# Wavelet attention: split lanes in both partition halves, and the row maxima as products of their own

## The reference, cut to what matters

```python
xe, xo = x[:, 0::2], x[:, 1::2]
a   = (xe + xo) * inv                      # (B, 1024, 128)
q   = (a @ wq).reshape(B, L, nh, hd)       # nh = 16 heads, hd = 8
k   = (a @ wk).reshape(B, L, nh, hd)
v   = (a @ wv).reshape(B, L, nh, hd)
att = einsum('bqhd,bkhd->bhqk', q, k) * (1 / sqrt(hd))
att = softmax(att, axis=-1)
o   = einsum('bhqk,bkhd->bqhd', att, v)
```

## Time and profile before

| | us |
|---|---|
| median of 3 runs | 4333.51 (4330.52 to 4335.92) |
| the profiled execution | 4323.26 |
| its span, first to last instruction | 4321.9 |
| TensorE busy, products | 3622.4 (84% of the span) |
| VectorE busy | 3291.8 (76%) |
| ScalarE busy | 2847.1 (66%) |
| GpSimd busy | 1003.8 (23%) |

### The profile page before, as it was taken

One profiled execution on the slowest core, in us unless ns is written; L12 is line 12 of the kernel. 1 busy time (PEld: TensorE's weight loads), 2 busy tenths in 40 slices (PEclk: granted clock), 3 DMA queues, 4 the chain that ended last, 5 costly groups with the idle time before them and its releaser, 6 DMA issues.

```text
span 4321.9 us, 74465 instructions
## 1 busy us (share of the span) xinstructions
PE 3622.4 (84%) x28950; PEld 1915.9 (44%) x28950; DVE 3291.8 (76%) x5099; ACT 2847.1 (66%) x4856; POOL 1003.8 (23%) x1479
## 2 busy tenths in 40 slices
PE   6999869998899998999996666666666659899999
PEld 4666522222444445676674122221122215566666
DVE  6787768886301137788886999999999996778887
ACT  3655416656334444666665999999999995566665
POOL 2444432100576630000002232322322220000000
PEclk8999959999999998999997555555555559899999
DMA  1000033330521000000001011111110110000000
GB/s 49 1 1 1 1 56 58 64 54 11 117 41 39 20 20 6 14 4 12 2 2 23 16 22 23 22 23 22 22 22 15 22 20 21 7 12 7 17 2 12
DMA packets 256877, 97.51 MB, mean 23 GB/s; under 512 B 223859, under 2 KB 241918, under 8 KB 256510
## 3 DMA queue, kind: packets, MB, share of 16 engines
q1 hardware_dynamic: 256526, 92.74, 10.8%
HBM read 31.75 MB, written 2.23 MB: 8 GB/s over the span
## 4 chain that ended last, share of the span: by engine, by line
PE 41%; DVE 29%; issue 12%; ACT 6%; DMA 1%; POOL 0%; SPq 0%; DVEq 0%; ACTq 0%; POOLq 0%
DVE d_negmax L2838 14%; PE psum L2364 7%; PE psum L2393 6%; DVE f_m_E L2463 6%; PE psum L2379 6%; PE psum L2063 5%; PE psum L2085 5%; ACT d_junk L2896 3%; PE psum L1447 2%; PE psum L1435 2%; DVE wl_negmax L1571 2%; DVE f_pT_E L2482 2%; PE psum L1424 2%; ACT wl_p L1712 1%; DVE residual L2493 1%
## 5 line engine op out<-in xcount | busy, mean ns | idle before, releaser
L2838 DVE TENSOR_REDUCE d_negmax<-psum 128x1 f32<-128x1024 f32 x1024 | 1171.5, 1214 | 25.5 <-PE psum L2774 23.4
L2896 ACT ACTIVATE d_junk<-psum,d_negmax 128x1024 bf16<-128x1024 f32 x1024 | 1136.8, 1126 | 37.0 <-DVE d_negmax L2838 32.6
L2774 PE MATMUL psum<-d_qT,d_kT 64*128 64x512 bf16 x2048 | 622.9, 604 | 432.7 <-ACT d_junk L2896 415.5
L2557 ACT ACTIVATE hidden<-psum,f_nm_E 128x1024 f32<-128x1024 f32 x512 | 566.5, 1113 | 143.5 <-DVE f_nm_E L2466 143.4
L2463 DVE TENSOR_REDUCE f_m_E<-psum 128x1 f32<-128x1024 f32 x512 | 602.1, 1218 | 46.8 <-PE psum L2364 45.5
L2364 PE MATMUL psum<-f_k_E,f_q_swapped_E 64*128 64x512 f32 x1024 | 527.2, 625 | 6.6 <-ACT hidden L2557 6.6
L2364 PE MATMUL psum<-f_k_E,f_q_E 64*128 64x512 f32 x1024 | 527.0, 624 | 2.9 <-DVE f_v_E L2454 2.0
L2564 ACT COPY f_pT_E<-psum 128x512 f32<-128x512 f32 x512 | 299.9, 586 | 323.8 <-PE psum L2379 323.8
L2393 PE MATMUL psum<-f_pT_E,f_v_E 128*64 128x128 f32 x8192 | 506.5, 277 | 2.5 <-DVE residual L2493 2.5
L2774 PEld LDWEIGHTS psum<-d_qT,d_kT 64*128 64x128 bf16 x2048 | 108.3, 101 | 843.1 <-ACT d_junk L2896 761.4
L2482 DVE COPY f_pT_E<-psum 128x512 f32<-128x512 f32 x512 | 351.6, 687 | 159.4 <-PE psum L2379 149.8
(11 more groups left out here) (331 smaller groups left out, 4720.9 us busy)
## 6 DMA issues: line engine op xcount, KB each, us to landing
moe_gates_on_all<-moe_gate_spill SPq DMA_DIRECT2D x16, 1024.0 KB, 11.8
f_q_swapped_E<-f_q_E SPq DMA_DIRECT2D x64, 128.0 KB, 2.3
moe_w<-in_moe_w SPq DMA_DIRECT2D x15, 256.0 KB, 6.5
residual<-in_hidden_states SPq DMA_DIRECT2D x2, 768.0 KB, 8.1
out<-residual SPq DMA_DIRECT2D x1, 1024.0 KB, 5.4
wl_qT<-wl_q_rows SPq DMA_TRANSPOSE x48, 3.3
residual<-in_hidden_states SPq DMA_DIRECT2D x2, 256.0 KB, 3.2
m_taps<-in_m_conv SPq DMA_DIRECT2D x4, 128.0 KB
```

What stands on the lines that cost most here:

```text
L2557: A.activation(pb[:, u % 2, f * 2 * BANK:(f + 1) * 2 * BANK], two(2 * f), ACT.Exp, bias=nm[:, u % 4:u % 4 + 1], scale=SC, accum_out=rs[:, ...
L2774: last = T.matmul(bank(2 + 2 * (at % 3) + jj), kT[half, s, jb * P:(jb + 1) * P], qT[half, s, hf * BANK:(hf + 1) * BANK], start=True, stop= ...
L2838: V.tensor_reduce(mh[:, t % 2, n // 2, n % 2:n % 2 + 1], two(2 + 2 * (at % 3)), X, ALU.max, negate=True).then_inc(*maxed.up(at))
L2896: A.activation(junk[:, at % 3, :], two(2 + 2 * (at % 3)), ACT.Exp, bias=mh[:, t % 2, n // 2, n % 2:n % 2 + 1], accum_out=sh[:, t % 2, n // ...
```

## The change

The ninth pair of parts (the two lowest, 2 and 2) is left out: `TERMS` has the eight pairs with i + j < 4, and `ROWS` is 64. The rows of q and k are laid out twice, in partitions 0 to 63 and 64 to 127 (index `r`), so `spread` makes 16 copies for q and 16 for k. The q rows have one buffer instead of two. In `pe_max` the first product of 512 columns takes the lower half, the second the upper half. In `pe_exp` the two products do the same and are left open, and two more products add the maxima: bf16 ones on three lanes against three lanes of `mT`, in the 32-partition group `(hh + 2 * j) % 4`, the two products of a unit in groups of opposite halves. The maxima's parts have their own tile `um`, which `dve_shift` fills (three small copies in place of one, to give the later half of the tokens a rotated order of heads) and `sp_shifted` transposes with one transposition into `mT`, two buffers. `dve_shift` no longer waits for the round's row transpositions but for the transposition of the maxima of the round before. GpSimd's memsets at the start fill other tiles. The waits follow: `pe_exp` waits once in a round for the maxima's lanes, `spread` for the row transpositions of the round before for q and k alike.

```diff
-        NG, HD, NH, ROWS = 9, 8, 16, 75
+        HD, NH, ROWS = 8, 16, 64
+        TERMS = [(i, j) for i in range(3) for j in range(3) if i + j < 4]
...
-                uq = sb(st, "wl_q_rows", [P, 2, 4, CT, P], BF16)
-                uk = sb(st, "wl_k_rows", [P, 4, CT, P], BF16)
+                uq = sb(st, "wl_q_rows", [P, 4, CT, 2, len(TERMS), HD], BF16)
+                uk = sb(st, "wl_k_rows", [P, 4, CT, 2, len(TERMS), HD], BF16)
+                um = sb(st, "wl_max_rows", [P, CT, 4, 32], BF16)
+                mT = sb(st, "wl_mT", [P, 2, B2], BF16)
+                onesb = sb(st, "ones_bf16", [P, P], BF16)
...
                     SP.wait_ge(*max_rows(b, g))
-                    if n:
-                        SP.wait_ge(*second_pass(*rounds_c[n - 1], 0, 3))
-                    for hh in range(4):
-                        SP.dma_start_transpose(in_lanes(qT[n % 3][:, hh]), in_blocks(uq[:, n % 2, hh])).then_inc(*shifted[hh].one())
+                    if n >= 2:
+                        SP.wait_ge(*second_pass(*rounds_c[n - 2], CT - 1, 3))
+                    SP.dma_start_transpose(in_lanes(mT[:, n % 2]), um[:, :, :, :].rearrange("p t g c -> p (t g c)")).then_inc(*shifted.one())
...
                     for j in range(2):
-                        last = T.matmul(bank(bk + j), qT[n % 3][0:ROWS, h % 4, i * P:(i + 1) * P], kT[n % 3][0:ROWS, h % 4, j * BANK:(j + 1) * BANK],
+                        half = slice(ROWS * j, ROWS * j + ROWS)
+                        last = T.matmul(bank(bk + j), qT[n % 3][half, h % 4, i * P:(i + 1) * P], kT[n % 3][half, h % 4, j * BANK:(j + 1) * BANK],
                                         start=True, stop=True)
...
                     for j in range(2):
-                        last = T.matmul(bank(bk + j), kT[n % 3][0:ROWS, hh, kt * P:(kt + 1) * P], qT[n % 3][0:ROWS, hh, j * BANK:(j + 1) * BANK], start=True, stop=True)
+                        half = slice(ROWS * j, ROWS * j + ROWS)
+                        T.matmul(bank(bk + j), kT[n % 3][half, hh, kt * P:(kt + 1) * P], qT[n % 3][half, hh, j * BANK:(j + 1) * BANK],
+                                 start=True, stop=False)
+                    for j in range(2):
+                        lanes = slice(32 * ((hh + 2 * j) % 4), 32 * ((hh + 2 * j) % 4) + 3)
+                        last = T.matmul(bank(bk + j), onesb[lanes, :], mT[lanes, n % 2, j * BANK:(j + 1) * BANK], start=False, stop=True)
...
-                    for i in range(3):
+                    for i, j in TERMS:
...
-                        for j in range(3):
-                            last = e.tensor_copy(u[:, :, :, i, j, :] if w == "q" else u[:, :, :, j, i, :], src)
+                        for r in range(2):
+                            last = e.tensor_copy(u[:, :, :, r, 3 * i + j, :], src)
...
-                    vstep(V.tensor_copy(mrest[:, :, :], negm[:, :, hs]))
-                    group_rows(V, round_at[b, g])
-                    places = uq[:, round_at[b, g] % 2].rearrange("p h t c -> p t h c")
+                    near, far = slice(0, CT // 2), slice(CT // 2, CT)
+                    V.tensor_copy(mrest[:, near, :], negm[:, near, hs])
+                    V.tensor_copy(mrest[:, far, 0:2], negm[:, far, 4 * g + 2:4 * g + 4])
+                    vstep(V.tensor_copy(mrest[:, far, 2:4], negm[:, far, 4 * g:4 * g + 2]))
+                    if round_at[b, g]:
+                        V.wait_ge(*max_turned(round_at[b, g] - 1))
```

More of the change, by code:

```diff
@@ L1292, in phase_C @@
                 turned = [loads(f"wl_turned_{n}") for n in range(2)]
-                shifted = [loads(f"wl_shifted_rows_{n}") for n in range(4)]
+                shifted = loads("wl_shifted_rows")
                 round_at = {r: n for n, r in enumerate(rounds_c)}
@@ L1302, in group_rows, with max_turned @@
                         e.wait_ge(*rows(n, hh))
-                def q_again(n, hh):
-                    return shifted[hh].sem, 16 * (n + 1)
+                def max_turned(n):
+                    return shifted.sem, 16 * (n + 1)
                 first_pass = signal("scored", at("max"))
@@ L1310, in phase_C @@
                 max_rows = signal("wl_max_rows", rounds_c)
+                lanes_set = signal("wl_lanes_set", range(1))
                 second_pass = signal("wl_shifted", at("exp"))
@@ L1326, in phase_C @@
                 in_lanes = lambda t: t.rearrange("p (t n) -> p t n", n=P)
-                in_blocks = lambda u: u.rearrange("p t c -> p (t c)")
+                in_blocks = lambda u: u.rearrange("p t r e x -> p (t r e x)")
                 def sp_rows(b, g):
@@ L1336, in sp_rows @@
                         arrived = turned[n % 2] if n else first_turned[hh]
-                        SP.dma_start_transpose(in_lanes(qT[n % 3][:, hh]), in_blocks(uq[:, n % 2, hh])).then_inc(*arrived.one())
+                        SP.dma_start_transpose(in_lanes(qT[n % 3][:, hh]), in_blocks(uq[:, hh])).then_inc(*arrived.one())
                         SP.dma_start_transpose(in_lanes(kT[n % 3][:, hh]), in_blocks(uk[:, hh])).then_inc(*arrived.one())
@@ L1429, in pe_exp @@
                     n = round_at[b, g]
-                    if kt == 0:
-                        T.wait_ge(*q_again(n, hh))
+                    if kt == 0 and hh == 0:
+                        T.wait_ge(*max_turned(n))
                     pe_av_behind(quad_at[b, g, kt], hh)
@@ L1523, in spread @@
                         e.wait_ge(*parted(b, 1, 2))
[L1524 to L1528, removed]
+                    if n:
                         group_rows(e, n - 1)
-                    u = (uq[:, n % 2] if w == "q" else uk[:, :, :, :])[:, :, :, 0:MR].rearrange("p h t (i j x) -> p h t i j x", i=3, j=3)
-                    for i in range(3):
+                    u = (uq if w == "q" else uk)[:, :, :, :, :, :]
+                    for i, j in TERMS:
                         cs = slice(D * (w == "k") + 4 * HD * g, D * (w == "k") + 4 * HD * (g + 1))
-                        src = part[:, i, :, cs].rearrange("p t (h x) -> p h t x", x=HD)
-                        for j in range(3):
-                            last = e.tensor_copy(u[:, :, :, i, j, :] if w == "q" else u[:, :, :, j, i, :], src)
+                        src = part[:, i if w == "q" else j, :, cs].rearrange("p t (h x) -> p h t x", x=HD)
+                        for r in range(2):
+                            last = e.tensor_copy(u[:, :, :, r, 3 * i + j, :], src)
                     return last
@@ L1575, in dve_shift @@
                     V.wait_ge(*maxed(b, 4 * g + 3, CT - 1))
-                    vstep(V.tensor_copy(mrest[:, :, :], negm[:, :, hs]))
-                    group_rows(V, round_at[b, g])
-                    places = uq[:, round_at[b, g] % 2].rearrange("p h t c -> p t h c")
+                    near, far = slice(0, CT // 2), slice(CT // 2, CT)
[4 more added lines that the diff above has]
+                        V.wait_ge(*max_turned(round_at[b, g] - 1))
+                    else:
+                        V.wait_ge(*lanes_set(0))
                     for n in range(3):
-                        last = V.tensor_copy(places[:, :, :, MR + n], mrest[:, :, :])
+                        last = V.tensor_copy(um[:, :, :, n], mrest[:, :, :])
                         if n < 2:
                             vstep(last)
-                            vstep(V.tensor_tensor(mrest[:, :, :], mrest[:, :, :], places[:, :, :, MR + n], ALU.subtract))
+                            vstep(V.tensor_tensor(mrest[:, :, :], mrest[:, :, :], um[:, :, :, n], ALU.subtract))
                     last.then_inc(*max_rows.up(b, g))
@@ L1736, in pool @@
                     enter(G)
-                    G.memset(uq[:, :, :, :, MR:P], 0.0)
-                    gstep(G.memset(uk[:, :, :, MR:P], 0.0))
+                    G.memset(onesb[:, :], 1.0)
                     for v in vp:
                         G.memset(v[:, :, :, HD:HD + 1], 1.0)
-                    gstep(G.memset(uk[:, :, :, MR:MR + 3], 1.0))
+                    G.memset(um[:, :, :, :], 0.0).then_inc(*lanes_set.up(0))
+                    G.wait_ge(*lanes_set(0))
                     for kind, *u in seq:
```

1 line of the change is left out of this document (removed).

## The result

| | before | after |
|---|---|---|
| median, 20 executions each on one chip | 4332.67 us | 4340.45 us |
| ratio, 95% interval | | 1.0017 (1.0011 to 1.0024) |
| span of the profiled execution | 4321.9 | 4339.9 |
| TensorE busy, products | 3622.4 | 3611.6 (83%) |
| GpSimd busy | 1003.8 | 1032.3 (24%) |

The change costs 7.8 us of the median, 0.17%, just inside what I called the same; the forecast was 10 us. The profiled pair differs by 18 us. Of these, 3.4 were there when the phase began (VectorE's first memset at 563.27 us instead of 559.88), which the change doesn't touch, and 4 came after its last copy of wl_oT; 10.4 us lie between these two marks.

What follows compares the result with a forecast made beforehand. The prediction took a quad's cycle of three E, three M, two AV and one maximum as the bound. It summed 1.2 + 4.2 + 2.4 + 2.4 = +10.2 us to 4344 us, range 4313 to 4385.

Steps and rivals of the forecast that it cites:

- what I called the same: Whole kernel: a measurement can tell about 0.2% from no change, 8.7 us; chance of landing within it 0.26.
- 40 quads: Five of eight wavelet attention rounds, four heads of one key tile each: 6.28 us against 6.25, together +1.2 us.
- last round, 8 quads: Last round, no M beside E: layout changes raise TensorE to 4.74 us against ScalarE's 4.21, together +4.2 us.
- copies at the start: Start of the phase: q and k layout copies grow from 9 to 16 each, seven more at 0.35 us, +2.4 us.
- maxima's lanes, 8 rounds: VectorE's step for each round: two more small copies ahead of its chain, 0.3 us a round, +2.4 us.
- The layouts: TensorE in wavelet attention: each change between row groups costs s = 0.11 us, bounds 0 to 0.20, two changes per E.
- the free layouts: Rival, TensorE: 64-row and 32-row groups coexist, s near 0, quad 5.67 us, total 4315 us; chance 0.30.
- 5.62 + 6s: Steady quad by the chain through the maximum, s per layout change: 6.28 us at s = 0.11, break-even at 0.105.
- lie in GpSimd's idle time: Later rounds' q and k copies, 11.2 us against 6.3, fit GpSimd's idle time; second round tightest, ready near 632.5, due near 634.
- No pairs: Rival, TensorE: pairs don't run side by side, M stays 0.44 us, E becomes 0.87 + 2s, above 4390 us; chance 0.05.
- Three-lane products in turn: Rival, products adding maxima in E run one after the other: 0.22 us more per E, 4382 us; chance 0.09.
- The clock: Rival: less streaming drops TensorE's clock to 0.50; 4402 us from two VectorE-heavy rounds, over 4550 in all; chance 0.09.

Runs made afterwards that it cites:

- One layout: Changed kernel with the maxima's parts also in 64 lanes, a ones-and-zeros matrix picking the head's rows: 4316.86 us, 0.9969 to the kernel before; again 4316.01, 0.9968.
- late-copies profile: Changed kernel with GpSimd's third-round k copies held until the first round's maxima are laid out: 4337.63 us, 1.0014 to the kernel before; again 4334.12, 1.0007.
- the kernel with both edits: Changed kernel with 64 rows for all E products and GpSimd's third-round copies held back: 4301.56 us, 0.9937 to the kernel before; again 4311.03, 0.9948.
- one layout and M in turn: Kernel with 64 rows for all E products, plus both products of each maxima pair on the same partition half: 4336.92 us, 1.0014 to the kernel before.

## Why the forecast came out right

The forecast was 4344 us and slower by 10; it measured 4340.45 and 7.8. The sum is right to 2 us, the terms less so:

| term | forecast | measured |
|---|---|---|
| 40 quads | +1.2 (6.28 us) | -0.8 (6.23) |
| last round, 8 quads | +4.2 (4.74 us) | +2.5 (4.52) |
| copies at the start | +2.4 | +2.4 |
| maxima's lanes, 8 rounds | +2.4 | 0 to +1.1 |
| small copy behind GpSimd | not seen | +5.9 |
| together | +10.2 | 10.0 to 11.1 |

The two rows of quads are a quad's difference times 40 and 8. By whole rounds of the profiled pair the five rounds are 0.1 us shorter, the last one is 2.3 longer (5.3 in the second profile of the changed kernel, with a lower clock), and rounds (0,0) and (1,0), which I had left as they are, are 1.1 shorter.

**The layouts** were the step that decided, and it held: s is 0.105 us against 0.11, taken from the earlier trace rows. It holds between 64 and 32 rows as well, which those rows didn't show; the argument for the free layouts fell. The trace agrees with the Trainium skill's rule on a drain ("TensorEngine Tiling (Array Packing)", Key Properties). 5.62 + 6s gives 6.25 us at that s, and 6.23 was measured. One layout gave 5.67 us, the free rival's quad, which shows that the layouts took the quad's gain. That its 4316 to 4317 us lie beside the rival's 4315 is partly luck: the rival's sum had no 5.9 us for the small copy and too many quads that gain 0.58.

**The last round** was mis-sized. I added 8s to two AV of 1.07 us, but that 1.07 already held the change from M's layout, 0.09 us. By rows it is 4 x (0.43 + 2 x 0.105) + 2 x 0.98 = 4.52. Nor are there eight such quads: the router's work and the clock lie between, and only one step from a quad's first exponential to the next's is 4.52 us, where before two were 4.21. That eight times 0.31 meets the whole round's 2.3 us is luck.

**The lanes** cost less than 0.3 us a round: the late-copies profile has the three copies 0.08 us apart, and its first cast comes 639.46 - 639.10 = 0.36 us behind their start, against 633.90 - 633.68 = 0.22 before. That is 0.14 us. Between rounds nothing of it shows: the first copies of wl_oT in four rounds one after another (712.91, 771.86, 822.86 and 873.86 us) lie 11.2, 11.6, 11.4 and 11.2 us later than before.

**That later rounds' copies "lie in GpSimd's idle time"** is the step that failed. I called the second round the tightest, worked out that its copies would end in time for TensorE, and didn't ask what VectorE does while the third round's run. These came across the shift in two ways. The longer copies of two rounds pushed the third's k copies from 623.56 us to 635.21, while the shift moved only from 633.68 to 639.97; and with one buffer for q its copies no longer stay behind 642.86 but follow at once. By the end of the k copies alone (640.75) the wait would have been about 0.8 us, an estimate. The forecast's total is right because this 5.9 us stands against three overestimates of together 5.0 to 6.1 us.

**The rivals.** No pairs: refuted by the records. Three-lane products in turn: didn't happen; made to happen they cost not 38 but 86 us, for the clock joined in. The clock: at 1.00 through the steady rounds as before, and my reason for the rival, that TensorE would stream too little, points the wrong way. The kernels in which it fell there stream more, not less. The 10.2 us from the profiled execution to the median was carried as forecast; by these 20 executions it is 9.4 for the kernel before, and for the changed kernel the profile lies 0.8 above its median.

## What to carry to other kernels

Before row groups of different sizes are packed side by side, count the changes between sizes on TensorE's path: here eight in a quad, six of them in the cycle that sets it, ate what halving the passes gave, and giving the small operand the large operand's layout, with a selection matrix, turned 0.17% slower into 0.3% faster, and with the late copies into 0.5% faster or more. When an edit lengthens or moves a GpSimd series, look up what VectorE does in that stretch, small copies too. A pass saved or added is priced at one clock; check in the profile that the clock is still there.

## What the runs showed of the hardware

A change between 64-row and 32-row groups costs 0.105 us (bf16, 512 columns), and 32-row groups in opposite halves run side by side, 0.39 us for a pair.

VectorE's copy of 128x16 or 128x32 took 6.24 to 6.59 us in all eight profiles with GpSimd's row copies beside it, and 0.17 to 0.18 where GpSimd stood still. The Trainium skill ("SBUF — State Buffer", Who interferes with whom) says that the two engines share a pair of ports as a lock, which in VectorE's two-port modes the one that issues first holds for a whole instruction. The trace agrees that one is blocked. But GpSimd's copies are 0.35 us each, and VectorE stood through about 18 of them, to the end of the series. In the fourth round of the kernel with both edits the same copy waited for one GpSimd instruction alone:

```profile
742.80 0.58 DVE L1585 COPY wl_negmax_rest<-wl_negmax 128x32 f32<-128x32 f32 x1
741.21 2.14 POOL L1562 TENSOR_TENSOR wl_q<-wl_q,wl_parts 128x1024 f32<-128x1024 f32 x1
```

It ends at 743.38 us, GpSimd's instruction at 743.35 and GpSimd's next, which needs its result, starts at 743.41. The copies of a series don't need one another's results and follow without such a gap; that this is why they let nobody in is likely, and no run was made for it. Where VectorE's copies began 0.1 us ahead of GpSimd's, at the start of the phase, the 16 of each ran through together in 5.38 and 5.54 us. Whether the order or their form (128x256 bf16, against 128x16 or 128x32 f32) makes this difference wasn't tried.

The granted clock fell to 0.50 in the middle of rounds in which TensorE was recorded busy 9.7 to 9.8 us of 10. With one layout and M in turn it stayed at 1.00 through 9.72 of 10 (880 to 890 us). Why is open.
